# The tails of the last two groups of a graph stage, moved into the first eight slots of the expert stage behind it

## What is computed

```python
def _L1_gnn_ref(x, adj, weight, w_ih, w_hh, b_ih, b_hh):
    ...
    for i in range(L):
        m = jnp.einsum('bnd,de->bne', h, weight[i])
        aggr = jnp.einsum('bst,bsd->btd', A, m)
        h = _gru_cell(aggr, h, w_ih, w_hh, b_ih, b_hh)
    return h

def _L1_ffn_ref(x, gate_w, gate_b, w1, w2, w3):
    ...
    logits = jnp.einsum('bsd,de->bse', x, gate_w) + gate_b
    probs = jax.nn.softmax(logits, axis=-1)
    top_probs, top_idx = jax.lax.top_k(probs, 2)
    top_probs = top_probs / jnp.sum(top_probs, axis=-1, keepdims=True)
    ...
    hidden = jax.nn.silu(h1) * h2
    expert_out = jnp.einsum('bseh,eho->bseo', hidden, w3)
    return jnp.einsum('bseo,bse->bso', expert_out, dispatch)
x = x + _L1_gnn_ref(_layernorm(x, axis=-1), adj, ...)
x = x + _L1_ffn_ref(_layernorm(x, axis=-1), ...)
```

## Time and profile before

| what | value |
|---|---|
| time, three runs | 1057.14, 1059.63 (median), 1060.46 us |
| the profiled execution | 1060.54 us, span of the core's instructions 1058.6 us |
| TensorE busy | 949.2 us, 90% of the span, 6368 matmuls |
| VectorE, ScalarE, GpSimd busy | 765.4 (72%), 554.1 (52%), 590.6 us (56%) |
| mean granted TensorE clock | 0.936 of 2.4 GHz |

### The profile page before, as it was taken

One profiled execution on the slowest core, in us unless ns is written; L12 is line 12 of the kernel. 1 busy time (PEld: TensorE's weight loads), 2 busy tenths in 40 slices (PEclk: granted clock), 3 DMA queues, 4 the chain that ended last, 5 costly groups with the idle time before them and its releaser, 6 DMA issues. The chain is left out here.

```text
span 1058.6 us, 24167 instructions
## 1 busy us (share of the span) xinstructions
PE 949.2 (90%) x6368; PEld 769.4 (73%) x6369; DVE 765.4 (72%) x2973; ACT 554.1 (52%) x1358; POOL 590.6 (56%) x623
## 2 busy tenths in 40 slices
PE   4776999999999997799999999999956899999970
PEld 3665999999989997455555555655536899999970
DVE  5557888888876666378898989989775555555558
ACT  4654665565553342355566655766533344444455
POOL 2155777777777755001356445564536777766670
PEclk9558999999999999799999999999986999999995
DMA  9611422222222422211303223040013543333349
GB/s 225 226 38 61 102 79 81 77 79 73 81 84 74 118 72 86 81 40 41 95 26 103 63 66 105 26 135 26 31 35 82 127 127 95 90 91 90 90 168 364
DMA packets 101512, 99.36 MB, mean 94 GB/s; under 512 B 32412, under 2 KB 86300, under 8 KB 101148
## 3 DMA queue, kind: packets, MB, share of 16 engines
q1 hardware_dynamic: 84252, 62.83, 21.4%
q0 software_dynamic: 17152, 35.29, 9.9%
HBM read 55.44 MB, written 42.62 MB: 93 GB/s over the span
## 5 line engine op out<-in xcount | busy, mean ns | idle before, releaser
L440 POOL DMA_INDIRECT queue<-rows,slots x256 | 259.0, 1012 | 161.5 <-issue 68.8
L2261 POOL DMA_INDIRECT result<-y_rows,y_ids x144 | 144.2, 1001 | 56.9 <-issue 48.3
L1026 POOL DMA_INDIRECT result<-y_rows,y_ids x136 | 134.8, 991 | 61.4 <-issue 35.7
L2292 PE MATMUL e_ps_h<-e_xT,e_up_of 128*128 128x128 f32 x1152 | 143.2, 278 | 2.7 <-DVE e_hT L2405 2.7
L2292 PEld LDWEIGHTS e_ps_h<-e_xT,e_up_of 128*128 128x128 f32 x1152 | 136.8, 195 | 3.5 <-issue 2.9
L1573 PEld LDWEIGHTS a_ps_y<-w_sb,a_hT 128*128 128x128 f32 x1088 | 131.1, 192 | 4.1 <-issue 1.3
L1573 PE MATMUL a_ps_y<-w_sb,a_hT 128*128 x1088 | 132.6, 275 | 1.1 <-DVE y_rows L1185 1.1
L1557 PE MATMUL a_ps_up<-a_xT,a_up_of 128*128 128x256 f32 x448 | 106.9, 381 | 1.1 <-DVE a_up_of L1156 0.8
L2405 DVE TENSOR_TENSOR e_hT<-e_ps_h,e_gate 128x512 f32<-128x512 f32 x72 | 49.7, 690 | 72.6 <-ACT e_gate L2340 70.9
L2340 ACT ACTIVATE e_gate<-e_ps_h 128x512 f32<-128x512 f32 x72 | 43.0, 597 | 96.8 <-PE e_ps_h L2292 95.5
L1557 PEld LDWEIGHTS a_ps_up<-a_xT,a_up_of 128*128 128x128 f32 x448 | 80.7, 190 | 11.8 <-issue 1.5
(11 more groups left out here) (287 smaller groups left out, 2071.4 us busy)
## 6 DMA issues: line engine op xcount, KB each, us to landing
xq<-queue SPq DMA_DIRECT2D x168, 64.5 KB
g_y<-result SPq DMA_DIRECT2D x20, 512.0 KB, 4.3
xq<-queue SPq DMA_DIRECT2D x56, 129.0 KB
result<-y_rows,y_ids POOLq DMA_INDIRECT x280, 2.3
x_res<-x SPq DMA_DIRECT2D x16, 256.0 KB, 3.9
w_sb<-w SPq DMA_DIRECT2D x2, 2048.0 KB, 12.0
queue<-rows,slots POOLq DMA_INDIRECT x256, 2.4
w_sb<-w SPq DMA_DIRECT2D x16, 256.0 KB, 4.0
```

The lines of the kernel that those rows point to most:

```text
L440: pool.indirect_dma_start(out=queue, out_offset=bass.IndirectOffsetOnAxis(ap=c.slots[q][:, k, t:t + 1], axis=0), in_=c.rows[q][:, k, t, :] ...
L1026: pool.indirect_dma_start(out=c.result0, out_offset=bass.IndirectOffsetOnAxis(ap=ids[slot.k][:, t, :].bitcast(U32), axis=0), in_=y[slot.k] ...
L2261: pool.indirect_dma_start(out=result, out_offset=bass.IndirectOffsetOnAxis(ap=ids[at_down.k][:, t, :].bitcast(U32), axis=0), in_=y[at_down ...
L2292: last = pe.matmul(ps_h[b][:, t, q * P:(q + 1) * P], up_of[at_up.k % 4][:, t, q * P:(q + 1) * P], xT[at_up.k % 4][:, t, :], start=True, st ...
```

## The change

The extra round of the graph stage goes: the tail now runs only for `1 <= n < pairs`. What the tail needs (its buffers, semaphores, and the functions `tail_back` to `tail_ids`, taken out of `gru_and_routing` with their bodies as they were) is allocated for both stages by `tail_of_gru`, and `experts` calls the functions between its first eight slots. The expert stage gives two PSUM banks to the tails, for all of its 72 pairs: `ps_x` and `ps_y` are single now. `gate` goes from four buffers to two. Sixteen slots are written out ahead of the loop, not eight; the tables of the remaining pairs and the single paddings move eight and ten slots later. The sigmoids of groups 14 and 15 move behind ScalarE's last slot, and `gap`, from which they are made, is held twice. GpSimd's 12 last row DMAs of groups 12 and 13, which ran in the extra round, now stand at the start of its expert program, with a wait for their landing behind them, and the row DMAs of groups 14 and 15 stand behind the scatters of pairs 1 and 3.

```diff
         def run_steps(eng, body):
             for n in range(-1, pairs + 1):
-                body(n, n + 1 < pairs, 0 <= n < pairs, n >= 1)
+                body(n, n + 1 < pairs, 0 <= n < pairs, 1 <= n < pairs)
...
-        gate = [sb(f"gate{b}", [P, PAIR, H1]) for b in range(4)] if layer else None
+        gate = [sb(f"gate{b}", [P, PAIR, H1]) for b in range(2)] if layer else None
...
-        ps_x = [pb(f"ps_x{b}", [P, 512]) for b in range(2)]
+        ps_x, ps_y = pb("ps_x", [P, 512]), pb("ps_y", [P, 512])
         ps_h = [pb(f"ps_h{b}", [P, PAIR, wide]) for b in range(2)]
-        ps_y = [pb(f"ps_y{b}", [P, 512]) for b in range(2)]
+        tail_banks(tail, pb("ps_m", [P, GN]), pb("ps_q", [P, GN]))
+        last = [At(NG // 2 - 1, b) for b in range(2)]
...
-            for k in range(UNROLL):
-                step(0, k)
-                if between:
-                    between(k)
-            with eng.Fori(1, known // UNROLL) as i:
+            for i in range(2):
+                for k in range(UNROLL):
+                    step(i, k)
+                    if between:
+                        between(i * UNROLL + k)
+            with eng.Fori(2, known // UNROLL) as i:
...
         def _(pool):
...
-            for group in late:
-                queue_rows(pool, c, queue, group % TURN)
+            def between(k):
+                if k == 5:
+                    rows_of(last[0])
+                if k == 7:
+                    rows_of(last[1])
+            even, odd = (At(NG // 2 - 2, b) for b in range(2))
+            rows_of(even, 4, 6)
+            rstd_and_shift(pool, c, tail.norm, tail.VT, tail.GT, tail.AT0, last[0])
+            rows_of(even, 6, 8)
+            rows_of(odd, 0, 2)
+            rstd_and_shift(pool, c, tail.norm, tail.VT, tail.GT, tail.AT0, last[1])
+            rows_of(odd, 2, 8)
             for q in range(2):
                 wait_landed(pool, c, q, 0)
-            steps(pool, body)
+            steps(pool, body, between=between)
...
         def _(pe):
...
-                    if not at_down.first(2):
-                        pe.wait_ge(y_copied, at_down.s * PAIR - PAIR)
+                    if not at_down.first(1):
+                        pe.wait_ge(y_copied, at_down.s * PAIR)
...
+            def between(k):
+                if k in (0, 1):
+                    if k:
+                        wait(pe, tail.VT, "x3", last[0].s)
+                    tail_back(pe, c, tail, last[k])
+                if k == 3:
+                    wait(pe, tail.VT, "x3", last[1].s)
+                    tail_turn(pe, c, tail, last[0])
+                if k in (4, 6):
+                    wait(pe, tail.VK, "carried", last[0].s - (k == 4))
+                    tail_score(pe, c, tail, last[k // 2 - 2])
+                if k == 4:
+                    tail_turn(pe, c, tail, last[1])
+                if k in (5, 7):
+                    route_tensor(pe, c, tail.r, tail.VS, tail.VK, tail.QT4, last[k // 2 - 2], E1)
...
         def _(act):
...
+            def tail_between(k):
+                if k in (2, 3):
+                    if k == 3:
+                        tail_rows(act, c, tail, last[0])
+                    norm_tail(act, c, tail, last[k - 2], counted)
+                if k == 4:
+                    tail_rows(act, c, tail, last[1])
...
-                steps(act, silu_body)
+                steps(act, silu_body, between=tail_between)
+                for at in last:
+                    tail_probs(act, c, tail, at)
+                wait(act, tail.AT2, "p1", last[1].s)
                 finish.scale(act)
...
         def _(v):
...
             def between(k):
-                if k == 4:
+                if k in (0, 1):
+                    tail_1(v, c, tail, last[k])
+                if k in (0, 2):
+                    tail_2(v, c, tail, last[k // 2])
+                    tail_ids(v, c, tail, last[k // 2], counted)
+                if k in (4, 6):
+                    route_vector(v, c, tail.r, tail.VS, tail.QT3, last[k // 2 - 2], E1, c.gate1_b[:], tail.QT4)
+                if k in (5, 7):
+                    route_vector_2(v, c, tail.r, tail.VK, None, tail.QT4, last[k // 2 - 2], E1)
+                if k == 12:
                     table_of_rest_1(v, c, table, experts_n)
...
                 steps(v, gated_body, 2, 4, between)
+                wait(v, tail.AT2, "p1", last[1].s)
                 finish.sum(v)
```

More of the change, by code:

```diff
@@ L415, in route_buffers @@
     r.slotf = sb(prefix + "slotf", [P, TOPK, G])
-    r.gap = sb(prefix + "gap", [P, G])
+    r.gap = [sb(prefix + f"gap{b}", [P, G]) for b in range(2)]
     r.egap = sb(prefix + "egap", [P, G])
@@ L1654, in make_edges, with tail_of_gru, sb, sem @@
     last.then_inc(c.VE.sem, 1)
-def gru_and_routing(nc, c, adj, weights, table):
+def tail_of_gru(nc, stage, c):
+    def sb(name, shape, dt=F32):
+        return stage.enter_context(nc.sbuf_tensor("l_" + name, shape, dt))
+    def sem(name):
+        return c.semaphore("l_" + name)
+    w = Shared()
+    w.norm = norm_buffers(sb, "tail")
+    w.state = [sb(f"state{b}", [D, GN]) for b in range(2)]
+    w.rT = sb("rT", [P, GN])
+    w.r = route_buffers(sb, None, sem, "q_", E1)
+    w.VT = Steps(sem("v_tail"), "x3 stats agg vare ids")
+    w.VS = Steps(sem("v_scores"), "scores top where wheref hot0 hot1 both")
+    w.VK = Steps(sem("v_ranks"), "ranked carried slot0 slot1 slots gap")
+    w.QT1, w.QT2, w.QT3, w.QT4 = (Steps(sem(f"q_tail{k}"), n) for k, n in enumerate(("back", "turned", "scored", "ranked")))
+    w.AT0, w.AT1 = Steps(sem("a_tail_norm"), "normed"), Steps(sem("a_tail_rows"), "rT rows_copied")
+    w.AT2 = Steps(sem("a_tail_probs"), "p0 p1")
+    w.GT = Steps(sem("g_tail"), "rstd shift")
+    return w
@@ new lines, in tail_banks, with tail_back, tail_turn @@
+def tail_banks(w, ps_m, ps_q):
+    w.ps_m, w.ps_rows = ps_m, [ps_q, ps_m]
+    w.r.ps_score = ps_q[:, 0:G * E1]
+    w.r.ps_rank = ps_q[:, G * E1:G * E1 + (G + 1) * E1]
+def tail_back(pe, c, w, at):
+    for t in range(G):
+        last = pe.transpose(w.ps_m[:, t * P:(t + 1) * P], w.state[at.b][:, t * P:(t + 1) * P], c.ident[:])
+    last.then_inc(w.QT1.sem, 1)
+def tail_turn(pe, c, w, at):
+    wait(pe, w.AT0, "normed", at.s)
+    for t in range(G):
+        last = pe.transpose(w.ps_rows[at.b][:, t * P:(t + 1) * P], c.rows[at.s % TURN][:, 0, t, 0:D], c.ident[:])
+    last.then_inc(w.QT2.sem, 1)
@@ new lines, in tail_score, with tail_rows @@
+def tail_score(pe, c, w, at):
+    wait(pe, w.AT1, "rT", at.s)
+    for t in range(G):
+        last = pe.matmul(w.r.ps_score[:, t * E1:(t + 1) * E1], w.rT[:, t * P:(t + 1) * P], c.gate1_w[:],
+                         start=True, stop=True)
+    last.then_inc(w.QT3.sem, 1)
+def tail_rows(act, c, w, at):
+    wait(act, w.QT2, "turned", at.s)
+    wait(act, w.QT3, "scored", at.back(1))
+    act.activation(w.rT[:], w.ps_rows[at.b][:], ACT.Copy).then_inc(w.AT1.sem, 1)
+    rows = c.rows[at.s % TURN]
+    act.activation(rows[:, 1, :, 0:D], rows[:, 0, :, 0:D], ACT.Copy).then_inc(w.AT1.sem, 1)
@@ new lines, in tail_1, with tail_2, tail_ids @@
+def tail_1(v, c, w, at):
+    wait(v, w.QT1, "back", at.s)
+    xs = c.x[:, bass.ds(at.s * G, G), :]
+    v.tensor_tensor(xs, w.ps_m[:].rearrange("p (t d) -> p t d", t=G), xs, ALU.add).then_inc(w.VT.sem, 1)
+def tail_2(v, c, w, at):
+    wait(v, w.VT, "x3", at.s)
+    statistics(v, c, w.norm, w.VT, w.GT, at)
+def tail_ids(v, c, w, at, counted=0):
+    if at.s >= TURN:
+        wait_landed(v, c, at.s % TURN, at.s // TURN - counted)
+    v.tensor_copy(c.rows[at.s % TURN][:, :, :, D:ROW].bitcast(I32),
+                  c.ids[:, :, at.s * G:(at.s + 1) * G].unsqueeze(3)).then_inc(w.VT.sem, 1)
@@ L1679, in gru_and_routing @@
         edges = c.edges
-        head_norm, tail_norm = c.head_norm, norm_buffers(sb, "tail")
+        head_norm, tail_norm = c.head_norm, w.norm
         xn = c.xn
-        state = [[sb(f"state{l}_{b}", [D, GN]) for b in two] for l in range(layers + 1)]
+        state = [[sb(f"state{l}_{b}", [D, GN]) for b in two] for l in range(layers)] + [w.state]
         tok = [sb(f"tok{b}", [P, G, D]) for b in two]
@@ L2134, in first, with experts @@
         return type(self.i) is int and self.s < n
-def experts(nc, c, layer, queue, result, experts_n, chunks, up, down, up_b, down_b, table, late, next_adj, finish):
+def experts(nc, c, layer, queue, result, experts_n, chunks, up, down, up_b, down_b, table, tail, next_adj, finish):
     pairs = tiles_of(experts_n) // PAIR
```

167 lines of the change are left out of this document (61 added, 106 removed).

## The result

The changed kernel took 1068.49 us in the median of three runs (1067.85 to 1070.28), the kernel before 1059.62 in the median of four beside it: ratio **1.008 [1.0063, 1.0097]**, so slower. (A fourth run of the changed kernel, 1174.57, fell in a slower state of the chip and is left out.) Its profiled run is the one of 1068.49, with a span of 1066.8 against 1058.6. The forecast was 1063.5 with a range up to 1069.0: the direction and the places were right, the size came to 8.2 us of span where the sum gave 3.9, and the time lies only 0.5 us inside the range.

A forecast was written before the change was run, and what follows sets the result against it. GpSimd's one-by-one DMAs were taken to bound the seam, TensorE the later slots, VectorE the finish. Expert stage +0.9 and end +3.0 gave +3.9 us; against the median of 1059.63 that made 1063.5 us, range 1059.6 to 1069.

The forecast's parts named there:

- First expert turn, T(8): TensorE's first expert turn at 789.4, 19.5 us earlier; its turn T(8) between bounds of 817.6 and 827.9.
- Its landing, to the first scatter: GpSimd's wait until group 13's last row DMA has landed, before the first scatter: taken as 3.7 us.
- 24 steps to the scatter of pair 4: On GpSimd, 4 scatters, 8 rows, 4 scatters and 8 rows, at 1.316 us each, before pair 4's first scatter.
- X: Time at which the first scatter of pair 4 starts on GpSimd: forecast 844.2, with bounds of 839.2 and 852.
- up(12), against 850.16: Start of pair 12's up on TensorE, which waits for pair 4's scatters: forecast 849.4, before 850.16.
- Half clock behind it: TensorE's first up after the wait for pair 4's scatters runs at about 1.2 GHz, losing 1.63 us.
- Expert stage: Net effect on the expert stage: +0.9 us, all of the lead given back at the scatter of pair 4.
- Drain of the single `ps_y`: At the end, the last three downs each wait for the copy before, 1.65 us a pair: +1.2 us.
- Table load and sigmoids: On ScalarE ahead of the first scaling, a 1.28 us table load and four sigmoids of some 0.5: +1.8 us.
- the line on GpSimd: GpSimd's indirect DMAs, one after another at 1.316 us each, bound the seam and delay the scatters TensorE waits for.
- 0.7 us a slot: Estimated cost per steady slot if single banks exposed each copy, by the skill's rule; the sum kept nothing.
- The rival with a longer wait on GpSimd: Slow landing or half-clock TensorE puts X at 847 to 851: +6.7 to +10.7 us, 1066 to 1070; chance 0.18.

## Why the prediction was right, and where its sizes were off

The steps, as the prediction made them, and what the runs showed:

| Step | Predicted | Measured |
|---|---|---|
| First expert turn, T(8) | 789.4; 817.6 to 827.9 | 789.55; 816.86 |
| Last row of group 13 | 808.9 | 809.77 |
| Its landing, to the first scatter | 3.7 | 5.05 |
| 24 steps to the scatter of pair 4 | 31.6 | 31.66 |
| X | 844.2 | 846.48 |
| up(12), against 850.16 | 849.4 | 851.81 |
| Half clock behind it | +1.6 | +2.5 |
| Expert stage | +0.9 | +4.44 |
| Drain of the single `ps_y` | +1.2 | +2.80, of it 0.8 at half clock |
| Table load and sigmoids | +1.8 | +1.94 |
| Behind the last addition | 0 | -1.0 |
| Span | +3.9 | +8.2 |

**Right**: that TensorE's 19.5 us don't matter, since the line on GpSimd decides; that its wait for landing is the unknown; that the scatter of pair 4 is the place where the lead ends; that nothing covers the end. The runs with the rows moved show it: with not one instruction of TensorE changed, T(71) comes 13.4 us earlier, 12.6 of it within the stage. The single banks were rightly put at nothing in the steady slots, and the Trainium skill, "Perfetto Trace Analysis", section Matmul Optimizations, which asks for all eight banks, is borne out only in the drain, 2.0 us without the half clock, where no other matmul covers the copy. The prediction's 0.7 us a slot, its price for that rule, is worked out from no row that it names, and the runs show nothing of it: 2.90 us a slot with one bank each and with two.

**Luck**: that the time stayed within the range, by 0.5 us, with four terms off; the 1.0 us less behind the last addition, which the sum didn't have, helped. T(8) came 0.7 us ahead of the earlier of its two bounds, which by the prediction's own terms (789.4 + 19.0 + 8 × 1.12) would have been 817.4 and not 817.6; nothing rested on it.

**The landing** was the first mis-sized term of the stage: 5.05 us, not 3.7, and 6.0 to 6.2 in three other runs. I took a time near that with free queues; the padding still ran, and without it the wait was 3.39. The 31.66 us of the next term look like a hit and are none: the steps took 1.262 and not 1.316, which saves 1.3 us, and a gap of 1.69 ahead of the second scatter took it back. That gap had a precursor before (1.63 us behind GpSimd's first DMA of the stage, between 809.17 and 811.76), which I had folded into no step.

**The clock** was the second. The sum charged one slow up, 1.63 us. From up(12) to the next up it took 5.44 us (851.81 to 857.25) where a slot takes 2.90: the up took 3.76 and the down behind it, 1.84, was slow too, at a mean granted clock of 0.56 (850 to 858), near the lower level of 1.2 GHz. Another 0.25 us was lost between there and T(71), in two slots of 3.04 and 3.01 us (from 883.12 and from 952.82).

**The drain** was the third. I took a cycle of 1.65 us for each of the last pairs; it took 1.97 (1028.05 to 1030.02), as it was 1.19 from down to copy rather than 1.10 and the hop from copy to down 0.33 rather than 0.1; with the last down at full clock the second cycle is 2.10 (in the run with early probabilities). Two such cycles make 2.0 us more than before. In the changed kernel half clock added 0.82 to the last one. The wait ahead of that down doesn't explain it alone: three runs have the same wait and full clock.

**Missed altogether**: the first wall, at up(10), 7.79 us. By the trace it costs nothing beside the second, since GpSimd's line ran through both without a gap and TensorE waited for it again at up(12); but the prediction spoke of one wall only. The rival with a longer wait on GpSimd needed X over 847; X stayed below, and yet the cost came into its range, by the clock and the drain.

Where a page bears on the step that decided: the Trainium skill, "DMA: Bandwidth & Descriptors", section Anatomy of one DMA, calls descriptor generation on GpSimd's path small and variable, and says that a lot of descriptors can be emitted before the incremental cost shows. If that were all that an issue costs, the lead would have been kept. The trace has 1.26 us for each indirect DMA of 128 rows (0.96 busy and 0.30 to the next), one after another, and these steps decided the time; how much of it is descriptor generation it doesn't tell.

## What to carry to other kernels

Before work is moved earlier, list what its results still have to queue behind: an engine that issues DMAs one by one is a line with one server, and each thing in it has a date; what is wanted late may stand in no place where something wanted soon comes after it, and no idle time ahead of the first urgent thing may go unused. A long stall on TensorE is to be charged with the slow instructions behind it, not only with the wait: the first ups behind stalls of 2.69 to 7.79 us took 3.55 to 3.76 us here, against 1.95. And a buffer that is halved has to be priced in the drain apart from the steady slots: there nothing else covers the copy.
